# The second score pair of the next head's second row tile, one slot later in a fused decoder kernel

## The reference, cut to what matters

```
q = (query @ Wq + bq).reshape(B, L, NKV, G, HDIM)            # B=4, L=256, NKV=8, G=4, HDIM=128
k_, v_ = jnp.split(kv @ Wkv + bkv, 2, axis=-1)               # 1601 context rows
scores = jnp.einsum('blkgd,bmkd->bkglm', q, k) * scale
attn = jax.nn.softmax(scores, axis=-1)
o = jnp.einsum('bkglm,bmkd->blkgd', attn, v).reshape(B, L, NHEAD * HDIM)
return o @ Wo + bo
```

## Time and profile before

| what | before |
|---|---|
| device time, median of 3 runs | 3160.7 us (3159.67 to 3161.76) |
| the profiled execution's own time | 3158.65 us |
| its span | 3156.9 us |
| mean granted TensorE clock | 0.990 |
| TensorE busy | 3027.7 us, 96% |
| VectorE busy | 1679.3 us, 53% |
| ScalarE busy | 1460.4 us, 46% |
| GpSimd busy | 344.5 us, 11% |

### The profile page before, as it was taken

How to read it: one execution, slowest core, us unless ns; L and a number is a source line. 1 busy time by engine, 2 the same in 40 slices (tenths; PEclk the granted TensorE clock), 3 DMA queues, 4 the chain that set the end, 5 groups by cost and what they waited for, 6 DMA issues and landing times.

```text
span 3156.9 us, 50348 instructions
## 1 busy us (share of the span) xinstructions
PE 3027.7 (96%) x19632; PEld 2710.1 (86%) x19632; DVE 1679.3 (53%) x3492; ACT 1460.4 (46%) x3368; POOL 344.5 (11%) x359
## 2 busy tenths in 40 slices
PE   7899999999889999999989999999988999999997
PEld 6798989897679898989768989898966898989895
DVE  5364646455637364646463737363646373736464
ACT  4453535344535353535463635353536353535353
POOL 3010101011101010101120101010102010101010
PEclk9999999999999999999999999999999999999999
DMA  3101010102210101010221010101022101010102
GB/s 124 64 1 43 25 41 28 41 28 71 89 58 1 67 1 47 21 41 28 77 86 54 1 67 1 67 1 52 17 84 79 54 1 67 1 67 1 67 1 90
DMA packets 39112, 138.67 MB, mean 44 GB/s; under 512 B 4320, under 2 KB 4448, under 8 KB 31456
## 3 DMA queue, kind: packets, MB, share of 16 engines
q1 hardware_dynamic: 38880, 135.46, 12.3%
HBM read 133.35 MB, written 2.10 MB: 43 GB/s over the span
## 4 chain that ended last, share of the span: by engine, by line
PE 77%; DVE 9%; issue 6%; ACT 5%; DMA 2%; POOL 0%; SPq 0%; ACTq 0%; DVEq 0%; POOLq 0%
PE bank L755 29%; PE sp L755 23%; PE dn L755 14%; PE bank L912 9%; DVE mneg L629 4%; ACT ph L500 2%; DVE ot L649 1%; DMA stage<-in_ctx_t 1%; ACT pn L432 1%; PE sp L826 1%; ACT pbuf L462 1%; DVE mb L635 1%; DVE pl L677 1%; DVE nmx L594 1%; PE sp L761 0%
## 5 line engine op out<-in xcount | busy, mean ns | idle before, releaser
L677 DVE TENSOR_TENSOR pl<-bank,ph 128x512 fp32r<-128x512 f32 (+1 forms) x896 | 581.2, 649 | 515.5 <-ACT ph L500 500.2
L500 ACT ACTIVATE ph<-bank 128x512 fp32r<-128x512 f32 (+1 forms) x896 | 494.5, 566 | 700.1 <-PE bank L912 699.2
L755 PE MATMUL dn<-ph,vh 128*128 128x256 f32 (+1 forms) x1664 | 542.7, 326 | 0.0
L912 PE MATMUL bank<-cst,pbuf 128*128 128x128 f32 (+1 forms) x3328 | 512.0, 273 | 0.6
L629 DVE TENSOR_REDUCE mneg<-sp 128x1 f32<-128x800 f32 (+1 forms) x512 | 492.4, 985 | 24.6 <-PE sp L755 23.2
L462 ACT ACTIVATE pbuf<-sp,mb 128x800 f32<-128x800 f32 (+1 forms) x512 | 470.0, 926 | 53.5 <-DVE mb L635 53.5
L755 PE MATMUL dn<-ph,vl 128*128 128x256 f32 (+1 forms) x1664 | 464.9, 279 | 0.0
L755 PE MATMUL dn<-pl,vh 128*128 128x256 f32 (+1 forms) x1664 | 464.3, 279 | 0.0
L912 PEld LDWEIGHTS bank<-cst,pbuf 128*128 128x128 f32 (+1 forms) x3328 | 397.2, 140 | 75.7 <-issue 57.5
L755 PE MATMUL sp<-kh,qh 128*128 128x400 f32 (+1 forms) x1024 | 378.5, 370 | 13.3 <-ACT pbuf L462 3.7
L364 POOL TENSOR_SCALAR ot<-ot,cst 128x256 f32<-128x256 f32 x128 | 118.3, 924 | 2377.3 <-DVE ot L649 2377.3
(11 more groups left out here) (122 smaller groups left out, 4467.9 us busy)
## 6 DMA issues: line engine op xcount, KB each, us to landing
stage<-in_wq SPq DMA_DIRECT2D x32, 1024.0 KB, 4.8
wob<-in_wo SPq DMA_DIRECT2D x128, 256.0 KB, 4.0
stage<-in_wkv SPq DMA_DIRECT2D x17, 1024.0 KB, 4.8
stage<-in_ctx_t SPq DMA_DIRECT2D x16, 800.5 KB, 4.4
wqk<-in_ws SPq DMA_DIRECT2D x17, 513.0 KB, 3.6
wos<-in_wso SPq DMA_DIRECT2D x5, 1026.0 KB, 7.9
wv<-in_ws SPq DMA_DIRECT2D x17, 256.0 KB, 2.8
wbt<-in_wb SPq DMA_DIRECT2D x4, 1024.0 KB, 6.4
```

The source lines that it names most:

```text
L500: nc.scalar.activation(ph[0:rows, (t * NS + k) % 3, 0:cols], bank[slot_at(n, s) % RING][0:rows, 0:cols], ACT.Copy).then_inc(hi_ok, 1)
L677: nc.vector.tensor_tensor(pl[0:rows, (t * NS + k) % 3, 0:cols], bank[slot_at(n, s) % RING][0:rows, 0:cols], ph[0:rows, (t * NS + k) % 3, 0 ...
L755: return nc.tensor.matmul(dst, lhs, rhs, start=first, stop=final)
L912: last = nc.tensor.transpose(bank[at_ring % RING][0:w, col:col + P], pbuf[:, n % 2, tb, i * P:i * P + w], ident)
```

## The change

The six matmuls of scores (1,1) move from slot 3 to slot 4. `S_SLOT` is read by TensorE and by VectorE, so the row maximum of the pair and the bias of row tile 1 move to slot 4 too. `EXP_SLOT`, and with it ScalarE's program, stays.

```
-S_SLOT = {0: ((0, 0),), 1: ((0, 1),), 3: ((1, 0), (1, 1))}
+S_SLOT = {0: ((0, 0),), 1: ((0, 1),), 3: ((1, 0),), 4: ((1, 1),)}
 EXP_SLOT = {2: 0, 5: 1}
```

## The result

The changed kernel takes 3204.4 us (median of 4 runs, 3200.7 to 3206.5), the kernel before beside it 3161.2 us (3159.7 to 3166.3). The ratio is 1.0133, 95% interval 1.0115 to 1.015, or 42 us more with 36 to 47. Forecast were 39 us more, 3199.9 us, with a range of 3189 to 3212 us. A second set of 4 runs gave 3203.7 us against 3163.1 us (median of 23) and again 1.0133 (1.011 to 1.0155).

What follows compares the result with a forecast made beforehand. TensorE was taken as the bound, held at tr0 by exp (1,0). A bias 0.79 us later less 0.45 us of slack, taken as 0.35 us, times 112 heads gives 39.2 us more: 3199.9 us, range 3189 to 3212 us.

Steps and rivals of the forecast that it cites:

- The bound and its releaser: Head loop: TensorE bounds; exp (1,0) releases tr0, so any delay of it delays TensorE equally, 0.35 us a head.
- The slack of 0.45 us: Before exp (1,0): the bias could come 0.45 us later unnoticed, because ph5 in ScalarE's queue holds that exponential.
- The steps on TensorE and VectorE: Slots 3 to 5: tr5 keeps its time, pl4 ends before scores (1,1), whose maximum's input is 1.15 us later.
- Rival 1: VectorE, slots 3 to 4: without overlap of neighbours it becomes the limit; 0.44 us a head, 3210 us; chance 0.10.
- Rival 2: Before exp (1,0): bias still in time, ph5 goes on holding the exponential; time stays at 3160.7 us; chance 0.04.
- Rival 3: Slot 3: TensorE's wait is for exp (0,1), and the move hides it; 36 us less, 3125 us; chance 0.03.
- Rival 4: TensorE's clock: longer stalls bring the 1.2 GHz level for a tenth of these heads; about 3270 us; chance 0.05.
- The sum: All head loops: 112 heads times 0.35 us, 39.2 us more, with nothing gained back in the loop.
- the upper bound: High end of the range: strict VectorE order plus a further 0.03 us, 0.46 us a head, 51.5 us, 3212 us.
- The wait at tr0: Weight load of tr0: idle about 0.52 us in place of 0.17; unnamed wait growing from 57.5 to about 97 us.

Runs made afterwards that it cites:

- experiment 2: Changed kernel, with the row maximum of row tile 1 pair 1 of heads 1 to 7 reading 401 of 801 columns: 3165.4 us, ratio 1.0007 to the kernel before.
- experiment 4: Kernel before, TensorE's order kept, but VectorE takes the maximum of scores (1,1) and the bias in slot 4, behind pl4: 3258.7 us, ratio 1.0304.
- experiment 5: Kernel before, with TensorE issuing scores (1,1) in slot 4 while VectorE keeps maxima and bias in slot 3, ahead of pl4: 3228.1 us, ratio 1.0204.
- experiment 7: Kernel before, with tr4 moved ahead of scores (1,0) in slot 3, all else in place: 3141.1 us, ratio 0.9932.
- experiment 3: Kernel before, with the same row maximum shortened to 401 of its 801 columns, as a control: 3165.5 us, ratio 1.0.
- experiment 6: Kernel before, with both score pairs of row tile 1 moved from slot 3 to slot 4: 3180.5 us, ratio 1.0055.
- experiment 1: The changed kernel run again without any edit, against the kernel before: 3203.7 us, ratio 1.0133.

## Why the prediction was right

**The bound and its releaser.** Right for both kernels. tr0 follows exp (1,0) by 0.11 to 0.12 us at all 112 places of each, and experiments 2 and 4 moved the time by moving only what exp (1,0) waits for. It is no general rule: in experiments 5 and 7 pl4 holds TensorE first.

**The slack of 0.45 us.** Experiment 3 made the bias earlier for nothing, so there is slack. Its size comes from the two profiles: measured from tr5, the bias is done at 1.44 in place of 0.65 us, 0.79 us later, and exp (1,0) starts at 413.24 - 411.77 = 1.47 in place of 1.13 us, 0.34 us later; the other 0.45 us is the slack. The earlier trace rows gave 1.48 us for the same steps in slot 1.

**The steps on TensorE and VectorE.** pl4 ended 0.05 us before the scores, where the working had 0.06 us, so TensorE sets the start of the maximum. Rival 1, VectorE in strict order, didn't come: pl4 starts at 411.20 while the maximum before it runs to 410.30 + 0.98 = 411.28, with about the overlap of the earlier trace rows. Experiment 6 shows how close it is, since there VectorE is the limit.

**The other rivals.** Rival 2 fell with the new wait for the bias. Rival 3 fell too: the score wait in slot 3 stayed, and it ends with exp (0,0). Rival 4 didn't come: the mean granted clock of the changed kernel is 1.00 from 335 to 500 us, a stretch of head loops, as it is in the kernel before.

**The sum.** 0.35 us a head was forecast and 0.34 us measured, 38 us over 112 heads. The measured change of 42 us (36 to 47) holds it. The sum put everything outside the head loops at nothing, and that part of the 42 us is no success of the forecast. The rest of the 47.8 us by which the two profiled spans differ lies outside the head loops, mostly in the stages between batch elements: 565.7 us against 557.8 us for the three, at a lower mean clock. This varies without the change as well (experiment 1), and nothing here shows another reason than chance for its size of some 4 us in the medians. I had set the sum against the median of three runs, which lay within 2 us; with 23 runs the kernel before spreads over 3154.6 to 3170.2 us. A slip in the upper bound changes nothing: 0.44 + 0.03 is 0.47 and not 0.46 us, which would end the range at 3213 us.

**Where the wording was off.** The wait at tr0 was forecast at 0.52 us under "issue", 97 us with the other unnamed ones. It is 0.58 us, under another name, and 65.2 + 38.3 = 103.5 us. tr0 waits 0.41 us longer than before, but its head is only 0.34 us longer. The difference is in the weighing of slot 6. From tr6 to its first matmul it took 408.08 - 407.92 = 0.16 us before and takes 413.04 - 412.91 = 0.13 us now, and the next one follows after 0.21 in place of 0.23 us; TensorE reaches tr0 that much sooner. pl4, which this weighing needs, ended at about 408.04 in the kernel before and now ends more than 1 us before it is needed (411.88 for 413.04). TensorE, this weighing in the kernel before and in the changed one:

```profile
407.92 0.38 PE L912 MATMUL bank<-cst,pbuf 128*65 128x128 f32 x2
408.08 0.39 PE L755 MATMUL dn<-ph,vh 128*128 128x256 f32 x1
408.31 0.28 PE L755 MATMUL dn<-pl,vh 128*128 128x256 f32 x1
```

```profile
412.91 0.38 PE L912 MATMUL bank<-cst,pbuf 128*65 128x128 f32 x2
413.04 0.37 PE L755 MATMUL dn<-ph,vh 128*128 128x256 f32 x1
413.25 0.28 PE L755 MATMUL dn<-pl,vh 128*128 128x256 f32 x1
```

Experiment 3 is the control for this: the slots of the kernel before, with pl4 done 0.3 us before tr6.

```profile
409.87 0.38 PE L913 MATMUL bank<-cst,pbuf 128*65 128x128 f32 x2
...
410.01 0.37 PE L756 MATMUL dn<-ph,vh 128*128 128x256 f32 x1
```

It takes 0.14 us there, and tr0's idle time is 0.23 us with the head as long as before. So pl4 held this weighing by some 0.05 us in the kernel before. Once it doesn't, TensorE waits that much longer at tr0 instead: 0.58 - 0.23 is the 0.35 us of the forecast.

## What to carry to other kernels

Moving work later on the bounding engine is free for that engine and still costs what its readers lose: add up the chain behind the moved piece to the next wait of the bounding engine, and subtract the slack that another queue covers. Do it for every reader: in experiment 5 the bias was no later than in the changed kernel, and pl4 cost another 24 us. A wait of the bounding engine can be filled with work whose move makes no reader later (the transposes of experiment 7), while delaying what others read costs. And look for the same sequence of steps elsewhere in the kernel: its measured length (0.35 us late) checks the sum of the parts (0.34 us, which is also what was measured).

## What the runs showed that I hadn't expected

One kernel's executions spread over 15.7 us (0.5%, 23 runs of the kernel before). The profiles show a place where such a spread arises: the same stage between batch elements took 183.7 us at a mean granted clock of 0.97 and 189.1 us at 0.94. Two profiles with equally long heads, the kernel before and experiment 3, differ by 10.2 us in their spans, 8.5 us of it in the three stages. What decides where the lower level falls in them was not tried. The named releaser of a weight load can be wrong: in the changed kernel it says `pl`, which had ended 0.57 us before.
